# Third attention: its band added by a TensorE product into the scores' bank, in place of a VectorE add

## The chip, the cores and the metric

The kernel runs on one core of a Trainium2 chip. The metric is the device time of one execution in microseconds. The engines are TensorE (PE; its weight loads have a row of their own, PEld), VectorE (DVE), ScalarE (ACT), GpSimd (POOL) and SyncE (SP), which only issues transfers here. Each engine works through its own queue in order; semaphores tie them together.

## What is computed

A chain of six layers on 1024 tokens of 128 channels: a neighbourhood attention, a routed attention with a convolution, the attention that is changed, a mixture of eight experts, a full attention, and a second mixture. The third layer of work, cut to what matters:

```python
def _L2_attn_ref(x, Wqkv, Wproj, bproj):        # HEADS = 4, HEAD_DIM = 32, WIN = 128, RADIUS = 32
    xw = x.reshape(-1, WIN, C)                  # eight windows of 128 tokens
    q, k, v = ...                               # from xw @ Wqkv
    attn = einsum('bhid,bhjd->bhij', q, k) * SCALE
    attn = attn + band                          # 0 where 0 <= i - j <= 32, else -inf
    attn = softmax(attn, axis=-1)
    out = einsum('bhij,bhjd->bhid', attn, v)
    return out.reshape(...) @ Wproj + bproj
...
t = t + _L2_attn_ref(_ln_t(t), ...)
t = t + _L2_ffn_ref(_ln_t(t), ...)
```

## The kernel before

Tokens lie in T = 8 tiles of 128 (P). All semaphores and orders are written out by hand, one block for each engine; `at(name, k)` is the semaphore and the count that a wait wants, `.then_inc` raises it. `ps` is the whole PSUM, eight banks of 512 fp32 columns. Names that begin with `n2_` belong to the third attention.

Each engine has a loop over a step s for it, software-pipelined by hand. A tile's window is the tile itself, so a tile needs one score product per head: 4 heads x 128 columns fill one bank, `ps[:, s % 2]`. In step s the engines do this, in this order:

- PE: scores of tile s (four products, each fp32, which the trace shows as eight instructions), transpose of the normalised output of tile s-4 (L1085), transposes of the probabilities of s-2 (`turn4`, L865), product of the turned probabilities with the values of s-3, projection of s-5. Products are recorded at the helper's line L855.
- DVE: adds the band to the scores of tile s, out of the bank into the SBUF buffer `pS` (four slots in `arena`) (L1666), and takes the negated row maxima of it, into `nmx` (L1669); then normalises s-3 (reciprocal L1495, product L1496), adds the projection of s-5 to the residual (L1682), and gathers statistics for the next norm.
- ACT: four exponentials, one for each head, in place in `pS` with the maximum as bias (L734); then the copy of the turned output of s-4 (L670) and of the turned probabilities of s-2 (L743). All three stand in one queue.
- POOL: makes the four masked copies of the queries of a tile (L531), two slots, so those of tile t wait for the scores of tile t-2.

The semaphore `n2_sr` told PE that the add had read a bank, so the scores of s waited for the add of s-2. `n2_nmx` tells ACT of the maxima, `n2_p` counts exponentials, `n2_pt` turned tiles.

`band` is a 128x128 fp32 table of 0 and -1e30, made by POOL early; `ident` is the fp32 identity. `kr` is a 128x4x1024 buffer of rounded fp32 (fp32r) that holds the gathered keys in the second attention and parts of the first mixture later. POOL's queue ahead of the third attention is: last parts of the second attention (`split_stacks("n1")`), roots for the norms (L433), a wait for the gathered keys, the ones columns of the values (L561), then the first root of this attention's norm.

Of the kernel before, what the change touches and what calls it, by code (L numbers as in the profile page):

```python
# [5 lines left out]
P = 128  # L6
# [9 lines left out]
ALU = mybir.AluOpType  # L16
ACT = mybir.ActivationFunctionType
AX = mybir.AxisListType
# [5 lines left out]
NH4, HD4 = 4, 32  # L24
# [5 lines left out]
HEADS = T * NH8  # L30
# [121 lines left out]
def build(nc, A, out):  # L152
    with ExitStack() as ctx:
# [10 lines left out]
        def S(name):  # L164

            name = PLACE.get(name, (name, 0))[0]
            if name not in sems:
                sems[name] = ctx.enter_context(nc.semaphore(name))
            return sems[name]

        def at(name, k):

            return S(name), PLACE.get(name, (name, 0))[1] + k

        ps = ctx.enter_context(nc.psum_tensor("ps", [P, 8, HALF], F32))


        ident = sb("ident", [P, P])
        ones = sb("ones", [P, P])
        upper = sb("upper", [P, P])  # L180
        band = sb("band", [P, P])
# [110 lines left out]
        fills = sb("fills", [P, 1, P])  # L292


        q_high, k_stack, q_low, k_high = (kr[:, i, :] for i in range(4))
        k_masked = qr[:, :, :, :].rearrange("p b h n -> p (b h n)")

# [99 lines left out]
        def _(pool):  # L397
# [160 lines left out]
            split_stacks("n1")  # L558
            token_root("ln2", 0)
            pool.wait_ge(*at("k_gathered", KV * T))  # L560
            pool.memset(vaug4[:, :, :, HD4:HD4 + 1], 1.0).then_inc(S("ones_cols"), 1)  # L561
            pool.wait_ge(*at("ones_cols", 3))
            token_root("na", 0)
# [67 lines left out]
        def _(act):  # L631
# [97 lines left out]
            for s in range(T + 6):  # L729
                if s < T:  # L730
                    act.wait_ge(*at("n2_nmx", s + 1))
                    for h in range(NH4):
                        v = pS[:, s % 4, P * h:P * h + P]
                        act.activation(v, v, ACT.Exp, bias=nmx[:, s, h:h + 1]).then_inc(S("n2_p"), 1)  # L734
                t = s - 4
                if 0 <= t < T:
                    o_copy("n2", t, 6)
                t = s - 2
                if 0 <= t < T:
                    act.wait_ge(*at("n2_pt", t + 1))  # L740
                    if t >= 4:
                        act.wait_ge(*at("n2_pv", t - 3))
                    act.activation(pT[:, t % 4, :], ps[:, 2 + t % 2, :], ACT.Copy).then_inc(S("n2_pta"), 1)  # L743
# [109 lines left out]
        def _(pe):  # L853
# [218 lines left out]
            for s in range(T + 6):  # L1072
                if s < T:
                    pe.wait_ge(*at("n2_qm", s + 1))
                    if s >= 2:
                        pe.wait_ge(*at("n2_sr", s - 1))
                    for h in range(NH4):
                        mm(ps[:, s % 2, P * h:P * h + P], qm[:, s % 2, h, :],
                           bT[:, P * s:P * s + P]).then_inc(S("n2_s"), 1)
                t = s - 4  # L1080
                if 0 <= t < T:
                    pe.wait_ge(*at("n2_o", t + 1))
                    if t >= 1:
                        pe.wait_ge(*at("n2_oT", t))
                    pe.transpose(ps[:, 6, 0:P], oK[:, t % 2, :], ident[:, :]).then_inc(S("n2_ot"), 1)  # L1085
                t = s - 2
                if 0 <= t < T:
                    pe.wait_ge(*at("n2_p", NH4 * (t + 1)))
                    if t >= 2:
                        pe.wait_ge(*at("n2_pta", t - 1))  # L1090
                    turn4(2 + t % 2, [pS[:, t % 4, P * h:P * h + P] for h in range(NH4)]).then_inc(S("n2_pt"), 1)
                t = s - 3
                if 0 <= t < T:
                    pe.wait_ge(*at("n2_pta", t + 1))
                    if t >= 2:
                        pe.wait_ge(*at("n2_o", t - 1))
                    for h in range(NH4):
                        ins = mm(ps[:, 4 + t % 2, 33 * h:33 * h + 33], pT[:, t % 4, P * h:P * h + P], vaug4[:, t, h, :])
                    ins.then_inc(S("n2_pv"), 1)
                t = s - 5  # L1100
                if 0 <= t < T:
                    pe.wait_ge(*at("n2_oT", t + 1))
                    if t >= 1:
                        pe.wait_ge(*at("n2_add", t))
                    mm(ps[:, 7, 0:P], oT[:, P * t:P * t + P], w2p[:, :]).then_inc(S("n2_proj"), 1)
# [256 lines left out]
        def _(dve):  # L1362
# [297 lines left out]
            for s in range(T + 7):  # L1660
                if s < T:
                    dve.wait_ge(*at("n2_s", NH4 * (s + 1)))
                    if s >= 4:
                        dve.wait_ge(*at("n2_pt", s - 3))
                    v = pS[:, s % 4, :].rearrange("p (h k) -> p h k", h=NH4)
                    dve.tensor_tensor(v, ps[:, s % 2, :].rearrange("p (h k) -> p h k", h=NH4),  # L1666
                                      band[:, :].unsqueeze(1).broadcast_to([P, NH4, P]), ALU.add).then_inc(S("n2_sr"), 1)
                    dve.wait_ge(*at("n2_sr", s + 1))
                    dve.tensor_reduce(nmx[:, s, 0:NH4], v, AX.X, ALU.max, negate=True).then_inc(S("n2_nmx"), 1)  # L1669
                t = s - 6  # L1670
                if 0 <= t < T:
                    dve.wait_ge(*at("n2_add", t + 1))
# [278 lines left out]
```

## Time and profile before

| | |
|---|---|
| runs of the kernel, us | 543.63, 554.05, 555.6 |
| median, us | 554.05 |
| profiled execution, us | 544.95 |
| its span in the trace, us | 543.2 |
| mean granted TensorE clock, share of full | 0.937 |
| third attention's loop in the trace, us from the span's start | 271.6 to 303.2 |

Times in the rows are microseconds from the start of the span, durations are microseconds unless marked ns. A matmul's duration includes its way through the array, so matmuls that follow each other overlap in the rows: the distance of two starts is what a product costs in a row of products. The granted clock is 1.00 for 2.4 GHz and 0.50 for 1.2 GHz.

### The profile page before, as it was taken

What the parts mean: (1) busy time and instruction counts of PE and PEld (TensorE: products, weight loads), DVE (VectorE), ACT (ScalarE), POOL (GpSimd) and SP (SyncE); (2) the same over time, 40 slices, a digit from 0 to 9 for tenths busy, and PEclk for the clock granted to TensorE, in tenths of its full rate; (3) what the DMA queues carried; (4) which work ended last, traced back from release to release, by engine and by line L of the source; (5) the groups of instructions that cost most, each with busy time, mean ns of one, the idle gap of its engine ahead of it and who ended that gap; (6) DMA issues with size and microseconds to landing.
All of it is one profiled execution on the core that took longest, in us unless ns stands there. A gap on an engine that the chain in (4) does not pass through costs nothing.

```text
span 543.2 us, 9959 instructions
## 1 busy us (share of the span) xinstructions
PE 480.2 (88%) x3712; PEld 366.2 (67%) x3712; DVE 342.8 (63%) x863; ACT 251.8 (46%) x471; POOL 129.4 (24%) x168
## 2 busy tenths in 40 slices
PE   4989999595999999987489789999999899979994
PEld 4267776233778677764278569999999654567983
DVE  3988887388967978996465753333312761367367
ACT  0859887173544755471065175455541213310630
POOL 7332244013512232322350231111200500021000
PEclk9999999699899999997698569999999999979998
DMA  8000000000000000070000000111111000000001
GB/s 287 7 2 2 1 3 1 0 2 2 0 1 1 2 2 1 2 311 1 0 1 2 1 21 1 39 47 59 50 40 40 19 1 0 2 0 1 1 1 39
DMA packets 4681, 13.49 MB, mean 25 GB/s; under 512 B 466, under 2 KB 1562, under 8 KB 4250
## 3 DMA queue, kind: packets, MB, share of 16 engines
q1 hardware_dynamic: 4634, 12.86, 6.9%
q8 instruction: 30, 0.49, 0.4%
q14 instruction: 17, 0.14, 0.1%
HBM read 12.34 MB, written 0.52 MB: 24 GB/s over the span
## 4 chain that ended last, share of the span: by engine, by line
PE 74%; DVE 16%; ACT 3%; issue 3%; POOL 2%; DMA 1%; DVEq 0%; POOLq 0%; ACTq 0%
PE ps L855 63%; PE ps L865 9%; DVE tabs L1403 2%; DVE st L1387 1%; POOL rstd L433 1%; DVE pT L1487 1%; DVE tabs L1429 1%; PE ps L952 1%; DMA xT<-in_xT_dram 1%; ACT arena L734 1%; DVE nmx L1669 1%; DVE arena L1666 1%; DVE mv L1393 1%; DVE kr L1554 1%; DVE nmx L1622 1%
## 5 line engine op out<-in xcount | busy, mean ns | idle before, releaser
L855 PE MATMUL ps<-kr,qr 128*128 128x512 f32 (+2 forms) x368 | 115.3, 418 | 8.5 <-DVE vaug L1469 4.3
L855 PEld LDWEIGHTS ps<-kr,qr 128*128 128x128 f32 x368 | 69.7, 195 | 27.0 <-issue 7.6
L865 PE MATMUL ps<-ident,arena 128*128 128x128 f32 x474 | 75.5, 275 | 3.0 <-DVE pT L1487 1.6
L865 PEld LDWEIGHTS ps<-ident,arena 128*128 128x128 f32 x474 | 57.8, 141 | 15.6 <-issue 2.7
L769 ACT ACTIVATE arena<-ps,first 128x512 f32<-128x512 f32 x64 | 42.7, 688 | 38.9 <-PE ps L855 38.8
L855 PEld LDWEIGHTS ps<-fw,arena 128*128 128x128 f32 x512 | 58.3, 192 | 0.6
L855 PE MATMUL ps<-fw,arena 128*128 128x128 f32 x512 | 58.3, 275 | 0.0
L1744 DVE SCALAR_TENSOR_TENSOR aK<-ps,cw,aK 128x128 f32<-128x128 f32 x64 | 18.0, 345 | 63.6 <-PE ps L855 63.6
L665 ACT ACTIVATE pT<-ps 128x512 f32<-128x512 f32 (+2 forms) x64 | 33.8, 528 | 51.3 <-PE ps L865 50.6
L717 ACT ACTIVATE arena<-ps,nmx 128x512 f32<-128x512 f32 x64 | 42.4, 687 | 14.4 <-DVE nmx L1622 14.3
L1622 DVE TENSOR_REDUCE nmx<-ps 128x1 f32<-128x512 f32 x64 | 43.5, 681 | 8.1 <-PE ps L855 7.9
L1487 DVE COPY pT<-ps 128x512 f32<-128x512 f32 (+2 forms) x64 | 38.6, 603 | 8.1 <-PE ps L865 7.7
L496 POOL TENSOR_TENSOR qr<-fw,mask 128x1024 fp32r<-128x1024 f32 x16 | 30.6, 1912 | 44.7 <-PE ps L855 32.7
L693 ACT ACTIVATE arena<-arena,nmx 128x384 f32<-128x384 f32 (+1 forms) x64 | 35.2, 581 | 5.8 <-DVE nmx L1520 5.8
L1520 DVE CUSTOM_DVE_ANT_0 arena<-ps,tabs 128x384 f32<-128x384 f32 (+1 forms) x64 | 32.6, 518 | 7.2 <-PE ps L855 7.2
L433 POOL TENSOR_TENSOR rstd<-ve,nhalf 128x4 f32<-128x4 f32 x14 | 14.2, 1013 | 95.3 <-DVE ve L1396 95.1
L855 PE MATMUL ps<-pT,tabs 128*32 128x128 f32 (+1 forms) x544 | 33.4, 294 | 0.8 <-ACT pT L665 0.8
L855 PE MATMUL ps<-kr 128*128 128x512 f32 x76 | 31.3, 499 | 1.0 <-ACT kr L832 1.0
L510 POOL TENSOR_TENSOR tabs<-vaug,ones 128x151 f32<-128x151 f32 x32 | 14.1, 439 | 70.0 <-PE ps L855 48.3
L653 ACT ACTIVATE pT<-ps,lowbias,islow 128x512 fp32r<-128x512 f32 x32 | 24.8, 777 | 2.9 <-PE ps L855 0.6
L865 PE MATMUL ps<-ident,tabs 128*128 128x128 f32 x48 | 10.7, 364 | 15.6 <-DVE tabs L1403 15.0
L1554 DVE CAST kr<-arena 128x512 fp32r x32 | 23.2, 734 | 1.9 <-issue 1.5
(264 smaller groups left out, 825.4 us busy)
## 6 DMA issues: line engine op xcount, KB each, us to landing
fw<-in_m_w_dram SPq DMA_DIRECT2D x2, 2048.0 KB, 11.1
fw<-in_m_w_dram SPq DMA_DIRECT2D x16, 256.0 KB, 2.9
convw<-in_convw_dram SPq DMA_DIRECT2D x1, 1600.0 KB, 11.1
rows<-in_rows_dram SPq DMA_DIRECT2D x1, 584.0 KB, 6.8
xT<-in_xT_dram SPq DMA_DIRECT2D x1, 512.0 KB, 3.6
out_dram<-aK SPq DMA_DIRECT2D x2, 256.0 KB, 2.3
w<-in_w_dram SPq DMA_DIRECT2D x1, 448.0 KB, 7.6
late<-in_late_dram SPq DMA_DIRECT2D x1, 360.0 KB, 11.5
```

Source lines behind the costliest of these rows:

```text
L496: pool.tensor_tensor(qr[:, t % 2, :, :].rearrange("p (g a) n -> p g a n", a=2), qst[:, :, P * t:P * t + P].unsqueeze(2).broadcast_to([P, 4 ...
L653: act.activation(pT[:, u % 4, :].bitcast(F32R), ps[:, u % 4, :], ACT.Identity, bias=lowbias[:, layer, a, k:k + 1], scale=islow[:, a:a + 1] ...
L665: act.activation(pT[:, m % 8, 0:w], ps[:, 4 + m % 2, 0:w], ACT.Copy).then_inc(S(f"{name}_pta"), 1)
L693: act.activation(v, v, ACT.Exp, bias=nmx[:, t, h:h + 1], scale=-1.0).then_inc(S("n0_p"), 1)
L717: act.activation(pS8[:, n % 8, :], ps[:, n % N1_S, :], ACT.Exp, bias=nmx[:, n // NH8, n % NH8:n % NH8 + 1]).then_inc(S("n1_p"), 1)
L769: act.activation(hid(e)[:, c // 2, HALF * (c % 2):HALF * (c % 2) + HALF], ps[:, c % 4, :], func, bias=col("L2_ffn_b1", FC * e + c // 2)).t ...
L855: return pe.matmul(dst, lhsT, rhs, start=start, stop=stop, skip_group_check=True)
L865: ins = pe.transpose(ps[0:rows, bank, cols * j:cols * j + cols], src, ident[0:cols, 0:cols])
L1487: dve.tensor_copy(pT[:, m % 8, 0:w], ps[:, 4 + m % 2, 0:w]).then_inc(S(f"{name}_ptd"), 1)
L1520: dve.tensor_tensor_reduce(arena_s(t)[:, h, 0:w], ps[:, s % 4, 0:w], tab[:, h, :, :].rearrange("p l j -> p (l j)"), -1.0, FMAX, ALU.add, A ...
L1554: dve.tensor_copy(kfil[:, t % 2, :, P * j:P * j + P], kst[:, :, bass.ds(r * P, P)]).then_inc(S("k_gathered"), 1)
L1622: dve.tensor_reduce(nmx[:, s // NH8, s % NH8:s % NH8 + 1], ps[:, s % N1_S, :], AX.X, ALU.max, negate=True).then_inc(S("n1_nmx"), 1)
```

## The change

The band comes into the scores' bank by a product of its own, ahead of the four score products, which now accumulate onto it: stationary operand an fp32r copy of the identity, moving operand an fp32r copy of the band read four times over (512 columns). DVE takes the maxima straight from the bank. ACT's exponentials read the bank and write `pS`, so it is ACT that now waits for the `pS` slot to be free (`n2_pt`), and PE's scores of s wait for the exponentials of s-2 in place of the add. The two fp32r copies are made by POOL in `kr`, once, after the last score product of the second attention.

```diff
+        ident_r = kr[:, 0, 0:P]
+        band_r = kr[:, 0, P:2 * P]
...
             token_root("ln2", 0)
             pool.wait_ge(*at("k_gathered", KV * T))
+            pool.wait_ge(*at("n1_s", HEADS))
+            copy(ident_r, ident[:, :]).then_inc(S("n2_band"), 1)
+            copy(band_r, band[:, :]).then_inc(S("n2_band"), 1)
+            pool.wait_ge(*at("n2_band", 2))
             pool.memset(vaug4[:, :, :, HD4:HD4 + 1], 1.0).then_inc(S("ones_cols"), 1)
...
                     act.wait_ge(*at("n2_nmx", s + 1))
+                    if s >= 4:
+                        act.wait_ge(*at("n2_pt", s - 3))
                     for h in range(NH4):
-                        v = pS[:, s % 4, P * h:P * h + P]
-                        act.activation(v, v, ACT.Exp, bias=nmx[:, s, h:h + 1]).then_inc(S("n2_p"), 1)
+                        act.activation(pS[:, s % 4, P * h:P * h + P], ps[:, s % 2, P * h:P * h + P], ACT.Exp, bias=nmx[:, s, h:h + 1]).then_inc(S("n2_p"), 1)
...
                     pe.wait_ge(*at("n2_qm", s + 1))
+                    if s == 0:
+                        pe.wait_ge(*at("n2_band", 2))
                     if s >= 2:
-                        pe.wait_ge(*at("n2_sr", s - 1))
+                        pe.wait_ge(*at("n2_p", NH4 * (s - 1)))
+                    mm(ps[:, s % 2, :], ident_r, band_r.unsqueeze(1).broadcast_to([P, NH4, P]), stop=False)
                     for h in range(NH4):
                         mm(ps[:, s % 2, P * h:P * h + P], qm[:, s % 2, h, :],
-                           bT[:, P * s:P * s + P]).then_inc(S("n2_s"), 1)
+                           bT[:, P * s:P * s + P], start=False, stop=h == NH4 - 1).then_inc(S("n2_s"), 1)
...
                     dve.wait_ge(*at("n2_s", NH4 * (s + 1)))
-                    if s >= 4:
-                        dve.wait_ge(*at("n2_pt", s - 3))
-                    v = pS[:, s % 4, :].rearrange("p (h k) -> p h k", h=NH4)
-                    dve.tensor_tensor(v, ps[:, s % 2, :].rearrange("p (h k) -> p h k", h=NH4),
-                                      band[:, :].unsqueeze(1).broadcast_to([P, NH4, P]), ALU.add).then_inc(S("n2_sr"), 1)
-                    dve.wait_ge(*at("n2_sr", s + 1))
-                    dve.tensor_reduce(nmx[:, s, 0:NH4], v, AX.X, ALU.max, negate=True).then_inc(S("n2_nmx"), 1)
+                    dve.tensor_reduce(nmx[:, s, 0:NH4], ps[:, s % 2, :].rearrange("p (h k) -> p h k", h=NH4), AX.X, ALU.max, negate=True).then_inc(S("n2_nmx"), 1)
```

## Rows read from the trace of the kernel before

**Rows 1.** The page's chain that ended last, by engine, shares of the span.

```profile
PE 74%; DVE 16%; ACT 3%; issue 3%; POOL 2%; DMA 1%; DVEq 0%; POOLq 0%; ACTq 0%
```

**Rows 2.** Two stretches: length, busy time of each engine, granted clock, DMA.

```profile
271.60:293.80 22.20, 18.34 (x152) 17.12 (x152) 14.46 (x34) 14.60 (x44) 7.45 (x8) 1.00 0.01 2
293.80:303.20 9.40, 8.77 (x35) 7.08 (x34) 4.09 (x20) 1.43 (x4) 1.02 (x1) 0.50 0.00 0
```

**Rows 3.** Timeline of PE: start, duration, engine, line, operation [idle before].

```profile
271.65 2.02 PE L855 MATMUL ps<-bT,arena 128*128 128x128 f32 x16 [0.99 <-DVE arena L1467]
...
278.71 1.08 PE L855 MATMUL ps<-arena,pT 128*128 128x33 f32 x8 [1.12 <-ACT pT L743]
279.62 1.14 PE L855 MATMUL ps<-bT,arena 128*128 128x128 f32 x8
...
281.95 1.14 PE L855 MATMUL ps<-bT,arena 128*128 128x128 f32 x8
283.83 0.30 PE L1085 MATMUL ps<-ident,oK 128*128 128x128 f32 x1 [0.73 <-ACT oT L670]
...
285.53 1.06 PE L855 MATMUL ps<-bT,arena 128*128 128x128 f32 x8
286.42 0.27 PE L1085 MATMUL ps<-ident,oK 128*128 128x128 f32 x1
...
286.97 0.98 PE L855 MATMUL ps<-arena,pT 128*128 128x33 f32 x8
287.78 0.47 PE L855 MATMUL ps<-late,oT 128*128 128x128 f32 x2
288.09 1.06 PE L855 MATMUL ps<-bT,arena 128*128 128x128 f32 x8
...
292.21 0.30 PE L1085 MATMUL ps<-ident,oK 128*128 128x128 f32 x1 [0.69 <-ACT oT L670]
...
298.28 1.76 PE L855 MATMUL ps<-arena,pT 128*128 128x33 f32 x8
```

**Rows 4.** Timeline of DVE in step 4, the same columns.

```profile
280.80 0.69 DVE L1666 TENSOR_TENSOR arena<-ps,band 128x512 f32<-128x512 f32 x1 [0.46 <-PE ps L855]
281.52 0.69 DVE L1669 TENSOR_REDUCE nmx<-arena 128x4 f32<-128x512 f32 x1
```

**Rows 5.** Timeline of ACT in step 4, the same columns.

```profile
282.24 1.28 ACT L734 ACTIVATE arena<-arena,nmx 128x128 f32<-128x128 f32 x4 [1.85 <-DVE nmx L1669]
283.43 0.26 ACT L670 ACTIVATE oT<-ps 128x128 f32<-128x128 f32 x1
283.58 0.58 ACT L743 ACTIVATE pT<-ps 128x512 f32<-128x512 f32 x1
```

**Rows 6.** Groups by form: busy us, mean ns of one, idle before.

```profile
L1622 DVE TENSOR_REDUCE nmx<-ps 128x1 f32<-128x512 f32 x64 | 43.5, 681 | 8.1 <-PE ps L855 7.9
L717 ACT ACTIVATE arena<-ps,nmx 128x512 f32<-128x512 f32 x64 | 42.4, 687 | 14.4 <-DVE nmx L1622 14.3
...
L734 ACT ACTIVATE arena<-arena,nmx 128x128 f32<-128x128 f32 x32 | 10.2, 390 | 8.7 <-DVE nmx L1669 8.6
...
L453 POOL TENSOR_SCALAR onesr<-ones 128x128 fp32r<-128x128 f32 x1 | 0.3, 295 | 0.0
```

**Rows 7.** Timeline of PE in the second attention: two of the convolution's products.

```profile
229.35 0.42 PE L855 MATMUL ps<-kv_high,convw_high 128*128 128x512 f32 x1
229.60 0.42 PE L855 MATMUL ps<-tabs_parts,convw_high 128*128 128x512 f32 x1
```

**Rows 8.** Timelines of POOL, PE and DVE at the second attention's end.

```profile
233.34 0.16 POOL L561 MEMSET arena<- 128x32 f32 x1
...
239.39 0.51 PE L855 MATMUL ps<-kr,qr 128*128 128x512 f32 x1
...
241.05 1.01 POOL L433 TENSOR_TENSOR rstd<-ve,nhalf 128x4 f32<-128x4 f32 x1 [7.54 <-DVE ve L1396]
...
242.09 0.34 DVE L1403 TENSOR_SCALAR tabs<-aK,mv,rstd 128x128 f32<-128x128 f32 x1
```

## The prediction, made before the changed kernel had run

> **What bounds the kernel now.** I read the page first, its chain that ended last, by engine [rows 1]. TensorE (PE) holds 74% of that chain, VectorE (DVE) 16%, ScalarE (ACT) 3%. So a microsecond taken from DVE is worth something only where DVE sits on the chain. The third attention (the loops that count `n2_...`) is such a place. The stretches [rows 2] show it in two pieces. From 271.6 to 293.8 us PE runs at the full clock (2.4 GHz) and is busy for 18.3 of 22.2 us. From 293.8 to 303.2 us, when the last tiles drain, it runs at half (1.2 GHz) and is busy for 8.8 of 9.4 us. The first piece is what the change can touch: eight steps, one tile each.
>
> Then I read the timeline of each engine in that stretch, because an average hides that the eight steps have different limits. PE's order within a step s is scores of tile s, turned output (`ot`) of s-4, turned probabilities of s-2, product with values (`pv`) of s-3, projection of s-5. From the starts in [rows 3] the pitches, back to back, are: scores 0.89 (285.53 to 286.42), `ot` and turn together 0.55 (to 286.97), `pv` 0.81 (to 287.78), projection 0.31 (to 288.09). Their sum, 2.56 us, is the pure PE work of a step. But the score products of steps 4 to 7 start at 279.62, 281.95, 285.53 and 288.09: 2.82 us apart on average. The difference is holes: PE waits 1.12 us for ACT's copy of turned probabilities (before 278.71), 0.73 us for ACT's copy of the turned output (before 283.83), and again 0.69 us (before 292.21). What is late each time is a copy that ACT has queued behind the four exponentials of its step, and these wait for DVE. In step 4 the scores start at 279.62, DVE adds the band at 280.80 and takes the maximum at 281.52 [rows 4], ACT's exponentials start at 282.24, the copy of the output follows at 283.43 and that of the turned probabilities at 283.58 [rows 5]. So two limits are close together: PE's own work (2.56) and, in about every second step, the line scores, add, maximum, exponentials, copy.
>
> **What the change removes.** Eight DVE adds of 128x512. One add delays the maximum by 0.72 us (280.80 to 281.52) [rows 4]. The maximum stays and now reads the bank instead of the SBUF copy. The trace has that form: 128x512 out of `ps` is 681 ns in the second attention, and the present one is 0.69 [rows 4, 6]. I take no difference. So each line to the exponentials gets 0.72 shorter at DVE.
>
> **What it adds to PE.** Eight products of one identity with 512 columns of band, rounded operands (fp32r). The nearest rows are the convolution's products, also fp32r, 128x128 by 512, with a weight load each: they start 0.25 us apart at the full clock, 229.35 and 229.60 [rows 7]. I take 0.26. Bounds: below, 0.11, the pitch of one of the eight 128-column parts of the scores (0.89 / 8) [rows 3], since 512 columns can't pass faster than 128; above, 0.42, the whole duration of such a product, if it overlapped with nothing [rows 7]. The product stands ahead of the scores, so it is on PE's own queue and on the line to the maximum: the line gets 0.72 - 0.26 = 0.46 us shorter, PE's step 0.26 longer, 2.82 us. That is exactly the average step that the trace shows with its holes. This is the centre of the forecast: the holes are filled with band.
>
> **What it moves.** The exponentials read the bank. ACT from `ps` in this loop: a copy of 128x128 is 0.26, one of 128x512 is 0.58 [rows 5]; the exponential of 128x512 from `ps` with the same bias operand is 0.687 [rows 6]. 0.687 - (0.58 - 0.26) = 0.37 us for 128 columns from the bank, against 0.39 from the arena [rows 6]. I take no change (bounds 0.26, the bare copy, and 0.39). The Trainium skill, page "VectorE: DVE Perf Modes", section "The TRN2 errata", gives ScalarE 224 cycles of fixed cost from SBUF and 172 from PSUM, so 52 cycles or 43 ns less for each of the 32 exponentials; by that estimate the line to the copies would be 0.17 us shorter still in a step. The rows agree in the sign and show about half of it.
>
> **The wait that is added.** Scores of s waited for the add of s-2; now band and scores of s wait for the exponentials of s-2. Behind that wait on PE stand all of the step: scores, `ot`, turn of s-2, `pv`, projection. The turn of s-2 needs the same exponentials anyway, so only the scores lose their lead. In steady steps they have no use for it: the exponentials of s-2 end about 2.5 us before PE comes to the scores of s. At the start they do. With the same start at 271.65 [rows 3], working through the queues with the durations above:
> Step 0: scores reach DVE at 273.07, exponentials 273.80 to 275.08. Step 1: exponentials 275.04 to 276.32. Step 2: band waits for the first exponentials and starts at 275.2 (before, these scores ran ahead without asking for ACT); maximum 276.62, exponentials 277.35 to 278.63, turned copy of tile 0 ends at 279.12, so `pv` of tile 0 starts at 279.2 (278.71 before: 0.5 us late). Step 4: band at 280.02, scores 280.28, maximum 281.46, exponentials 282.2 (282.24 before), copies 283.38 and 283.53. Step 5: band 282.55, `ot` 283.78 (283.83 before), `pv` 284.33, projection 285.15. Step 6: band 285.46, scores 285.72, `ot` 286.61, projection 287.97. Step 7: band 288.28 (scores at 288.09 before), scores 288.54, `ot` 289.43, because its copy (288.99) is now in time; `pv` 289.98, exponentials of tile 7 end 291.65, its `ot` of tile 4 at 291.96 against 292.21 before.
> Sum of the loop: -0.25 us. Five band products lie on PE's own path (steps 3 to 7): at 0.42 each the sum is +0.55, at 0.11 it is -1.0.
>
> **The wait that is moved.** ACT now waits for the turn of tile s-4 before it writes the arena; that turn was issued two steps earlier, so it costs nothing. POOL makes the two rounded 128x128 copies before the ones columns and the third attention's first root. A POOL copy 128x128 to fp32r is 295 ns [rows 6]. It waits for the last score product of the second attention, which starts at 239.39 and lasts 0.51 [rows 8], so it runs from about 240.0 to 240.65; the memset (0.16, at 233.34 before) ends about 240.85, and the root starts at 241.05 in any case, because it waits for DVE [rows 8]. Cover: 0.2 us of slack. If it is gone, up to 0.3 us passes on, since DVE's first normalised tile starts at 242.09, right behind that root [rows 8]; the query splits come some 19 us later and their bias adds later too. PE's wait for the two copies ends 31 us before it is reached. I take 0.05 for POOL.
>
> **The sum.** -0.25 + 0.05 = -0.2 us: 544.95 becomes 544.75 for the profiled execution (span 543.2 and 1.75 around it). The runs shown are 543.63, 554.05 and 555.6: the median lies 9.1 us above the profiled execution, which is near the lowest. No row tells what makes the two levels, so I carry the difference over: 554.05 - 0.2 = 553.8 us.
>
> **Rivals.** A, the full saving reaches the end: 8 x 0.46 = 3.7 us, and the drain, where PE needs 1.67 us a tile at the full clock (0.55 + 0.81 + 0.31) but about twice that at half [rows 2, 3], keeps the full clock, some 3.5 us more. 554.05 - 7.2 = 546.9. For it: all the holes end on ACT behind DVE. Against: PE's own 2.82 a step stands in the way, and the clock fell at 293.8 in the first step without score products, which is still there. Chance 0.08.
> B, the lost lead costs more than the start: if semaphores and copies eat the margin, each of the steps 2 to 7 is held 0.3 to 0.7 us by exponentials of s-2. That is 2 to 4 us, 557. Against: the closed line of a tile, 0.26 + 1.09 + 0.73 + 1.28 + 0.1 = 3.5 us, serves two steps, 1.75 each, far below 2.82. Chance 0.12.
> C, the other side: the clock. PE now has holes of about 1.1 and 0.8 us near 274 and 278.4. If the clock falls there, as it fell at 293.8 after the first step without score products, and stays down, a step costs twice its 2.8 us: `pv` takes 1.76 instead of 0.98 [rows 3]. From four such steps on (11.2 us) the kernel is slower by over 2%; five make 14 us, 568. Against: a hole of 1.12 us stood there before [rows 3], and the clock held. Chance 0.05, of which 0.03 beyond four steps.
> The forecast itself, within 1.5 us of -0.2: 0.75.
>
> **Range and chances.** The mechanism alone gives 552.3 to 555.3 on the median's level. The two levels of the runs weigh more: if the median falls on the lower, 543.6 + the same. So the range is 542.8 to 557.0, which takes in B and A. Two per cent, about what a measurement of this kernel can tell from no change, is 11 us, more than half of the loop that is touched; only C or a change of level between the two kernels' runs gets there. Faster by over 2%: 0.04; within 2%: 0.91; slower by over 2%: 0.05.
>
> **What would show it.** Right: the score products' starts of steps 4 to 7 stay some 2.8 us apart with the holes before `ot` gone; the band product's pitch 0.25; the maximum 0.68 from the bank; first `pv` some 0.5 us later; DVE's busy time down by about 5.5 us and the end of the loop within 1 us. Wrong: steps of 2.6 us or less (A), holes before the band product in steps 4 to 7 (B), a granted clock of 0.5 before 290 us (C), or the root on POOL later than 241.4.

## The result

| | before | changed |
|---|---|---|
| median of 20 runs each, us | 545.03 (542.22 to 555.6) | 543.5 (539.41 to 555.0) |
| ratio | | 0.996, 95% interval 0.9943 to 0.9978 |
| profiled execution, us | 544.95 | 542.79 |
| its span, us | 543.2 | 541.0 |
| DVE busy, us | 342.8 | 337.4 |
| PE busy, us | 480.2 | 479.4 |

By these runs the changed kernel is 0.4% faster, 1.2 to 3.1 us, where the forecast was -0.2 us, no change. How much of that is the change's own is what the experiments are about. 543.5 us lies inside the stated range, and the kernel stays within 2%, but it moved, and the forecast said it would not. The ratio leaves out the longest executions of both kernels; the three of these that were traced (555.19 for the kernel before, 554.0 and 553.12 for the changed one) all show a long fall of the clock between about 440 and 464 us, which is the upper level of the three runs shown ahead of the prediction.

```profile
440.00:464.50 24.50, 24.50 (x44) 0.51 0.00 0
```

That is one stretch of such an execution of the kernel before: length, PE's busy time, granted clock 0.51 where it is 1.00 otherwise.

The loop of the changed kernel, PE's timeline (start, duration, operation, idle before):

```profile
270.17 0.47 PE L862 MATMUL ps<-kr 128*128 128x512 f32 x1 [0.94 <-issue]
...
273.58 0.47 PE L862 MATMUL ps<-kr 128*128 128x512 f32 x1 [0.93 <-ACT arena L741]
...
277.40 1.08 PE L862 MATMUL ps<-arena,pT 128*128 128x33 f32 x8 [0.46 <-ACT pT L750]
278.31 0.47 PE L862 MATMUL ps<-kr 128*128 128x512 f32 x1
278.62 1.05 PE L862 MATMUL ps<-bT,arena 128*128 128x128 f32 x8
...
280.87 0.48 PE L862 MATMUL ps<-kr 128*128 128x512 f32 x1
...
283.44 0.47 PE L862 MATMUL ps<-late,oT 128*128 128x128 f32 x2
283.66 0.47 PE L862 MATMUL ps<-kr 128*128 128x512 f32 x1
283.97 1.05 PE L862 MATMUL ps<-bT,arena 128*128 128x128 f32 x8
284.86 0.27 PE L1095 MATMUL ps<-ident,oK 128*128 128x128 f32 x1
...
286.44 0.48 PE L862 MATMUL ps<-kr 128*128 128x512 f32 x1
...
290.03 0.30 PE L1095 MATMUL ps<-ident,oK 128*128 128x128 f32 x1 [0.56 <-ACT oT L676]
```

`ps<-kr` is the band product. It starts at 278.31 in step 4, 280.87, 283.66 and 286.44 in step 7. Step 4 has no projection yet and takes 2.56 us; the two after it, which are whole steps, take 2.79 and 2.78. The holes ahead of the turned outputs in steps 5 and 7 [rows 3] are gone. What remains is a hole of 0.93 us before the third band product, the lost lead, and 0.46 and 0.56 us at both ends. DVE and ACT of step 4:

```profile
279.71 0.69 DVE L1673 TENSOR_REDUCE nmx<-ps 128x4 f32<-128x512 f32 x1 [0.69 <-PE ps L862]
```

```profile
280.44 1.14 ACT L741 ACTIVATE arena<-ps,nmx 128x128 f32<-128x128 f32 x4 [1.54 <-DVE nmx L1673]
281.46 0.29 ACT L676 ACTIVATE oT<-ps 128x128 f32<-128x128 f32 x1
281.61 0.62 ACT L750 ACTIVATE pT<-ps 128x512 f32<-128x512 f32 x1
```

The maximum from the bank takes 0.69 as before [rows 4]. The four exponentials take 1.14 us where they took 1.28 [rows 5]; one is 368 ns on average where it was 390 [rows 6], and they follow each other more closely too:

```profile
L741 ACT ACTIVATE arena<-ps,nmx 128x128 f32<-128x128 f32 x32 | 9.1, 368 | 8.9 <-DVE nmx L1673 8.9
```

Counted from its first product, the loop compares so (us; `ot` is the turned output, tile 4's is the first after the last scores):

| | forecast | changed | before |
|---|---|---|---|
| band or scores of step 4 | 8.37 | 8.14 | 7.97 |
| band or scores of step 7 | 16.63 | 16.27 | 16.44 |
| `ot` of tile 4 | 20.31 | 19.86 | 20.56 |
| last projection | | 29.78 | 30.69 |

So the loop gives 0.9 us. The two profiled spans differ by 2.2, and most of the rest stands ahead of the loop: it starts at 270.17 instead of 271.65 [rows 3], behind code that is the same but for POOL's two copies. The experiments begin with that.

### The profile page after: what moved, and what is told of

It reads as the page before. It is cut to its first block, busy times and chain, and to the rows that moved or that the text cites. A ratio compares the mean times of both kernels' runs of the same rounds, so it can differ in the third digit from the quotient of the medians.

```text
span 541.0 us, 9969 instructions
## 1 busy us (share of the span) xinstructions
PE 479.4 (89%) x3720; PEld 366.5 (68%) x3720; DVE 337.4 (62%) x855; ACT 251.1 (46%) x471; POOL 130.2 (24%) x170
## 4 chain that ended last, share of the span: by engine, by line
PE 73%; DVE 16%; ACT 3%; issue 3%; POOL 2%; DMA 1%; DVEq 0%; POOLq 0%; ACTq 0%
PE ps L862 63%; PE ps L872 9%; DVE tabs L1413 2%; DVE tabs L1439 2%; DVE st L1397 1%; POOL rstd L435 1%; DVE pT L1497 1%; PE ps L959 1%; DMA xT<-in_xT_dram 1%; ACT arena L741 1%; DVE mv L1403 1%; DVE kr L1564 1%; ACT arena L699 1%; DVE nmx L1632 1%; DVE st L1378 1%
## 5 line engine op out<-in xcount | busy, mean ns | idle before, releaser
L498 POOL TENSOR_TENSOR qr<-fw,mask 128x1024 fp32r<-128x1024 f32 x16 | 30.7, 1918 | 44.1 <-PE ps L862 32.6
L862 PE MATMUL ps<-kr 128*128 128x512 f32 x84 | 35.1, 497 | 2.9 <-ACT kr L839 1.0
L862 PEld LDWEIGHTS ps<-kr 128*128 128x128 f32 x84 | 15.3, 187 | 17.9 <-issue 14.7
```

The costliest lines, as they stand in the source:

```text
L498: pool.tensor_tensor(qr[:, t % 2, :, :].rearrange("p (g a) n -> p g a n", a=2), qst[:, :, P * t:P * t + P].unsqueeze(2).broadcast_to([P, 4 ...
L862: return pe.matmul(dst, lhsT, rhs, start=start, stop=stop, skip_group_check=True)
```

## The experiments

The changed loop and three theories were put to the test. M: the gain is the loop's alone, and the rest of the 2.2 us is the clock, which differs from execution to execution. N: there is a real gain outside the loop. P: after the change PE's own work limits steps 3 to 7; its rival Q, that the line over DVE and ACT still does.

**The two kernels again.** No edit.

> The changed kernel once more, beside the kernel before on one chip. Theory M (the gain is made in the third attention's loop alone, where the traces show 29.8 us from its first product to its last projection against 30.7): ratio 0.997 to 0.9995, 0.3 to 1.5 us. Rival N (there is a real gain outside the loop too, since the twenty runs gave 0.996, 2.2 us): 0.994 to 0.997. In the trace: band product on PE adds 0.22 us to the pitch of a step, four exponentials 1.14 us.

> The kernel before, once more, as one of the kernels compared, for the scatter of the times and for the clock. Theory K (the start of the loop and the clock in its drain differ from execution to execution of the same code): ratio 0.996 to 1.004; loop from first product to last projection 30.7 us if the clock falls about 22 us into it, 28.0 us if it holds, as it did with the copies alone. Rival (the drain's clock is set by the kernel): 30.7 us and a fall at 22 us again.

Measured: the changed kernel 0.9935 (0.9878 to 0.9992), the kernel before against itself 1.0012 (0.9984 to 1.004). The interval of the first holds both theories. The trace of the kernel before settles the start of the loop:

```profile
270.21 2.02 PE L855 MATMUL ps<-bT,arena 128*128 128x128 f32 x16 [0.99 <-DVE arena L1467]
```

It starts at 270.21, where the changed kernel's stood at 270.17. This execution took 543.45 us against 542.79: at an equal start the difference is 0.7 us, not 2.2. The clock is part of the cause of the two starts: in this execution, as in the changed kernel's, it is down from 251.4 to 254.8 us, in the first one of the kernel before from 249.4 to 256.3. But that gives only the last 0.5 of the 1.44 us. The same product, first execution and this one:

```profile
246.74 1.08 PE L855 MATMUL ps<-pT,tabs 128*32 128x128 f32 x32 [0.78 <-ACT pT L665]
```

```profile
245.80 1.08 PE L855 MATMUL ps<-pT,tabs 128*32 128x128 f32 x32 [0.78 <-ACT pT L665]
```

0.94 us stand between the two here already, and 0.47 at 93 us (93.51 and 93.04 for one product), before the clock's first fall in these traces, near 98 us. So the start is no work of the change, as M said, since two executions of one kernel show both; but only part of it is the clock's. That the drain would keep the clock at times is not seen here: the clock fell 22 us into the loop and the last projection started 30.74 us into it, as the rival said of this execution.

**The two copies alone.** Into the kernel before:

```diff
             pool.wait_ge(*at("k_gathered", KV * T))
+            pool.wait_ge(*at("n1_s", HEADS))
+            copy(ident_r, ident[:, :]).then_inc(S("n2_band"), 1)
+            copy(band_r, band[:, :]).then_inc(S("n2_band"), 1)
+            pool.wait_ge(*at("n2_band", 2))
```

> The kernel before with only POOL's wait and its two rounded copies added, used by nobody. Theory M: they are hidden, 0 to +0.3 us, and the first root of the third attention's norm starts within 0.1 us of where it did (241.05), measured from the second attention's last score product (239.39). Rival N, that the new wait shifts POOL's work and so gives the gain outside the loop: -0.5 to -1.3 us.

Measured 0.9991 (0.995 to 1.0031), the median 545.32 against 545.52: no gain, no loss. The first root of the norm starts 1.67 us after the second attention's last score product (243.07 and 241.40), where it was 1.66 before, as M said. In the changed kernel's own timeline of POOL the copies take 0.31 each, and the root then still idles 0.18 us for DVE:

```profile
239.13 0.31 POOL L455 TENSOR_SCALAR kr<-ident 128x128 fp32r<-128x128 f32 x1 [6.79 <-PE ps L862]
239.41 0.31 POOL L455 TENSOR_SCALAR kr<-band 128x128 fp32r<-128x128 f32 x1
239.77 0.16 POOL L567 MEMSET arena<- 128x32 f32 x1
240.11 1.01 POOL L435 TENSOR_TENSOR rstd<-ve,nhalf 128x4 f32<-128x4 f32 x1 [0.18 <-DVE ve L1406]
```

This trace gave something else: its loop, the same code as before, started at 272.92, kept the full clock through the drain and reached its last projection 28.04 us in, against 30.7. So the drain's clock is worth 2.65 us in the loop, and the kernel does not fix it: the second half of M. At the end of this execution 1.6 of them were gone again, though. From the last projection to the end it took 244.15 us, where the two executions of the kernel before took 242.61 and 242.50: the clock fell once more, from 328.9 to 332.3 us, in the first mixture, and stayed down longer near 480.

**The move without the product.** DVE still adds the band, in place in the bank:

```diff
-                    v = pS[:, s % 4, :].rearrange("p (h k) -> p h k", h=NH4)
-                    dve.tensor_tensor(v, ps[:, s % 2, :].rearrange("p (h k) -> p h k", h=NH4),
+                    v = ps[:, s % 2, :].rearrange("p (h k) -> p h k", h=NH4)
+                    dve.tensor_tensor(v, v,
                                       band[:, :].unsqueeze(1).broadcast_to([P, NH4, P]), ALU.add).then_inc(S("n2_sr"), 1)
```

with ACT's and PE's waits and the exponentials' source as in the change.

> DVE still adds the band, but in place in the bank; maximum and exponentials read the bank, scores of s wait for the exponentials of s-2. It has the move of the change without PE's product. Theory M1, that the exponentials from the bank were the part of the gain that the forecast left out: four exponentials take 1.14 instead of 1.28 us, each hole of PE behind them shrinks by 0.14, the lost lead costs 0.3 to 0.6 at the start; loop -0.5 to +0.3 us against before. Rival M2, the lost lead costs in every step: steps of 2.9 us or more, loop +1 to +3 us.

Measured 0.9999 (0.9954 to 1.0043). PE and ACT:

```profile
275.27 1.13 PE L856 MATMUL ps<-bT,arena 128*128 128x128 f32 x8 [1.89 <-ACT arena L735]
276.23 0.88 PE L866 MATMUL ps<-ident,arena 128*128 128x128 f32 x4
...
282.92 1.14 PE L856 MATMUL ps<-bT,arena 128*128 128x128 f32 x8
284.68 0.30 PE L1086 MATMUL ps<-ident,oK 128*128 128x128 f32 x1 [0.62 <-ACT oT L670]
```

```profile
275.31 1.14 ACT L735 ACTIVATE arena<-ps,nmx 128x128 f32<-128x128 f32 x4 [0.19 <-DVE nmx L1668]
```

The exponentials take 1.14 here as well, so that gain belongs to reading the bank. The hole of step 5 is 0.62 instead of 0.73 [rows 3], and the steps 4 to 7 start 2.33, 3.47 and 2.55 us apart, against 2.33, 3.58 and 2.56: M2, a cost in every step, falls. The sum of M1 (-0.5 to +0.3 us) can't be read from this trace, because the clock fell inside the loop. The lost lead is bare here, a hole of 1.89 us before the scores of step 2, because add and maximum still stand one behind the other; with the band on PE it is 0.93. In this execution the clock fell to half right behind that hole, from 276.4 to 279.8 us. That is how rival C of the prediction begins, in a kernel with a hole of 1.9 us; it came back after 3.4 us and did not reach C's four steps. It was seen once, and in none of the eight traces of the changed kernel, with 0.93. The execution took 550.61 us: it also had a fall from 440 to 457 us.

**The product twice.** Into the changed kernel:

```diff
                     mm(ps[:, s % 2, :], ident_r, band_r.unsqueeze(1).broadcast_to([P, NH4, P]), stop=False)
+                    mm(ps[:, s % 2, :], ident_r, band_r.unsqueeze(1).broadcast_to([P, NH4, P]), start=False, stop=False)
```

> The changed kernel with the band product issued twice into the same bank (the mask is -2e30 then). Theory P, PE is the limit of steps 3 to 7 after the change and a band product costs its pitch: 0.21 to 0.26 us more a step, loop +1.2 to +2.0 us against the changed kernel. Rival Q, PE still has slack in the loop and the line over DVE and ACT limits it: +0.2 to +0.6 us.

Steps 6 and 7 of it (the two products are one row, x2), and the first hole after them:

```profile
284.72 0.70 PE L862 MATMUL ps<-kr 128*128 128x512 f32 x2
285.26 1.05 PE L862 MATMUL ps<-bT,arena 128*128 128x128 f32 x8
...
287.73 0.70 PE L862 MATMUL ps<-kr 128*128 128x512 f32 x2
...
291.54 0.30 PE L1096 MATMUL ps<-ident,oK 128*128 128x128 f32 x1 [0.56 <-ACT oT L676]
```

The step is 3.01 us, 0.23 more than 2.78, and the turned output of tile 4 starts 21.23 us into the loop, 1.37 later: theory P, six times 0.23 (the first two products stand in the start's holes). The whole kernel did not show it: 0.9974 (0.9929 to 1.0019), median 543.96. In this trace the clock held through the drain and the last projection came at 28.56 us, earlier than the 29.78 of the changed kernel. From there to the end it took 244.08 us against 242.84, again with a fall near 327 us.

**The product left out.** The changed kernel without the band product, so the mask is missing from the computation.

```diff
-                    mm(ps[:, s % 2, :], ident_r, band_r.unsqueeze(1).broadcast_to([P, NH4, P]), stop=False)
...
-                           bT[:, P * s:P * s + P], start=False, stop=h == NH4 - 1).then_inc(S("n2_s"), 1)
+                           bT[:, P * s:P * s + P]).then_inc(S("n2_s"), 1)
```

> The changed kernel without the band product: the mask is left out of the computation, everything else (maximum and exponentials from the bank, waits) stays. Theory P (PE is the limit after the change): each of steps 3 to 7 is 0.22 us shorter, the turned output of tile 4 starts 0.9 to 1.6 us earlier in the loop than with the band (19.86 us into it). Rival Q (the line over DVE and ACT limits it): 0.2 us or less there, with holes before the turned outputs in place of the band.

```profile
285.93 1.06 PE L862 MATMUL ps<-bT,arena 128*128 128x128 f32 x8
...
288.49 1.06 PE L862 MATMUL ps<-bT,arena 128*128 128x128 f32 x8
```

The step is 2.56 us, PE's pure work without the band, and the turned output of tile 4 starts 18.55 us in: 1.31 earlier. P again, from the other side. The line over DVE and ACT has room for 2.56. Ratio to the kernel before 0.9948 (0.9907 to 0.9988). The traced execution, 548.64 us, kept the clock in the drain and had a fall from 438.5 to 455.5 us.

**Both.** The kernel before with the product added, and DVE still adding the band.

```diff
                         pe.wait_ge(*at("n2_sr", s - 1))
+                    mm(ps[:, s % 2, :], ident_r, band_r.unsqueeze(1).broadcast_to([P, NH4, P]), stop=False)
                     for h in range(NH4):
                         mm(ps[:, s % 2, P * h:P * h + P], qm[:, s % 2, h, :],
-                           bT[:, P * s:P * s + P]).then_inc(S("n2_s"), 1)
+                           bT[:, P * s:P * s + P], start=False, stop=h == NH4 - 1).then_inc(S("n2_s"), 1)
```

> The kernel before with the band product added on PE, and DVE still adding the band and writing the arena (mask -2e30): the cost side of the change alone. Theory M: the product lies on the line of a step and in PE's own work, so the turned output of tile 4 starts 0.7 to 1.8 us later in the loop than before (20.56). Rival R (the forecast's picture that the product only fills holes): 0.3 us or less.

```profile
290.20 0.30 PE L1094 MATMUL ps<-ident,oK 128*128 128x128 f32 x1 [0.28 <-ACT oT L676]
...
292.98 0.30 PE L1094 MATMUL ps<-ident,oK 128*128 128x128 f32 x1 [0.92 <-ACT oT L676]
```

The turned output of tile 4 starts 21.49 us in, 0.92 later than in the kernel before: theory M. R falls. The holes in front of the turned outputs stay, because the product lengthens the line just as it lengthens PE's work. What fills the holes in the change is not the product; it is that DVE's add and part of the exponentials leave the line. From this kernel to the changed one the same mark moves from 21.49 to 19.86: 1.6 us is what the DVE add and the SBUF reads were worth, and 0.9 is what the product costs. The difference is the loop's 0.7. The kernel's time shows nothing of the cost, 0.9995 (0.9966 to 1.0025); its loop too kept the clock in the drain.

**The drain filled.** The changed kernel with two idle products in each drain step, into a bank nobody reads:

```diff
+                elif s < T + 6:
+                    if s < T + 2:
+                        pe.wait_ge(*at("n2_p", NH4 * (s - 1)))
+                    for _ in range(2):
+                        mm(ps[:, s % 2, :], ident_r, band_r.unsqueeze(1).broadcast_to([P, NH4, P]))
```

> The changed kernel with two more products of identity and band in each of the six drain steps, into a bank that nobody reads. Theory K2: they keep PE busy, the clock stays at its upper level through the drain, and the last projection starts 27 to 29 us into the loop instead of 29.8; ratio to before 0.990 to 0.996. Rival: the clock falls at 22 us all the same, the products then cost up to 0.9 us a step, last projection at 31 to 34 us.

> The changed kernel with the filled drain once more: three of its seven timed executions took 539.5 to 539.8 us, the profiled one 542.65 with its loop starting at 273.2. Theory K: an execution of 539.5 to 540.6 us starts its loop near 270.2 and reaches the last projection 27.2 us later. Rival: the loop start is elsewhere, and the short executions gain outside the loop.

Measured 0.9929 (0.991 to 0.9949, seven executions) against the kernel before, 3.9 us, median 540.58: the fastest of all. In both traces the clock holds and the last projection starts 27.17 and 27.18 us in. The second execution took 540.8 us and its loop started at 271.41, so the theory of a start near 270.2 is not borne out by it; the changed kernel in an execution that started at 271.43 took 543.93. The drain of the two, changed kernel first:

```profile
292.68 0.47 PE L862 MATMUL ps<-late,oT 128*128 128x128 f32 x2
293.44 0.40 PE L1095 MATMUL ps<-ident,oK 128*128 128x128 f32 x1 [0.30 <-DVE oK L1506]
293.64 1.06 PE L872 MATMUL ps<-ident,arena 128*128 128x128 f32 x4
294.49 1.76 PE L862 MATMUL ps<-arena,pT 128*128 128x33 f32 x8
```

```profile
292.90 0.71 PE L862 MATMUL ps<-kr 128*128 128x512 f32 x2
293.44 0.32 PE L1100 MATMUL ps<-ident,oK 128*128 128x128 f32 x1
293.60 0.60 PE L872 MATMUL ps<-ident,arena 128*128 128x128 f32 x4
294.04 0.98 PE L862 MATMUL ps<-arena,pT 128*128 128x33 f32 x8
```

Both turn an output at 293.44. The idle products sit in a hole, and the product with the values behind it takes 0.98 instead of 1.76.

**The same in the kernel before.** Into the kernel with the two copies alone:

```diff
+                elif s < T + 6:
+                    if s < T + 2:
+                        pe.wait_ge(*at("n2_sr", s - 1))
+                    for _ in range(2):
+                        mm(ps[:, s % 2, :], ident_r, band_r.unsqueeze(1).broadcast_to([P, NH4, P]))
```

> The kernel before (band added by DVE) with the same two products in each drain step, and the two copies on POOL that they need. Theory M: the clock holds, last projection 28.0 us into the loop; ratio to before 0.994 to 0.997, and the changed kernel with the filled drain stays 0.7 to 1.2 us faster than this one. Rival N (the changed loop has a further gain of over 1 us apart from the drain's clock): 2 us or more between the two.

Measured 0.9981 (0.9962 to 0.9999). The clock held, the last projection came 28.05 us in. In the loops the two filled kernels differ by 0.87 us (28.05 and 27.18), the same as the unfilled ones. But the ratio misses M's 0.994 to 0.997: here the same products bring 1 us, in the changed kernel 3. Against their kernels before the two filled kernels stand at 0.9929 and 0.9981, 2.8 us apart, each with an interval of about 1.1 us to either side, where M said 0.7 to 1.2. That speaks for more than the loop in the timed runs, as N said. The traces place part of it behind the loop: from the last projection to the end this kernel took 243.58 us, the changed one 242.32 and 242.21, and near 480 us the clock was down for 10.2 us here (478.4 to 488.6) and for 6.8 us there. That is one trace; why the fall was longer is not shown.

**Filled as far as the first mixture.** In addition 28 products of 256 columns ahead of PE's waits for the next norms:

```diff
+            warm(6, 5)
             for i in range(2):
...
+                warm(5, 5)
...
             router("m2", 0, 4, oT, "nb_T", range(4, T))
+            warm(12, 5)
```

> The kernel with the filled drain, and 28 products of 256 columns on operands that lie there anyway, put before PE's waits for the next norms and for the first mixture. Theory K2: the clock stays at its upper level from 270 to the first mixture's products, whose first 5 us ran at the lower one; 2 to 4 us less than with the filled drain alone, ratio to before 0.984 to 0.990. Rival: the products delay the turns, or the clock falls between the bursts; within 1 us of the filled drain (0.993).

Measured 0.9971 (0.9944 to 0.9998), 2.3 us slower than the filled drain alone, though the two intervals meet: neither theory's ratio. The clock did hold at 1.00 from the loop to beyond 330 us, and still the mixture did not start earlier:

```profile
298.33 2.75 PE L862 MATMUL ps<-first 128*128 128x256 f32 x12
...
308.64 5.43 PE L862 MATMUL ps<-first 128*128 128x256 f32 x24
313.72 1.51 PE L862 MATMUL ps<-kr,qr 128*128 128x512 f32 x5
```

Six such products take 2.75 us, 0.46 each, and twelve 5.4. The mixture starts 16.15 us after the last projection, instead of 13.2 to 13.3 with the filled drain alone and 13.6 without: the filling outlasted the waits. The idea is not refuted by it; a filling of half the size was not run.

**More executions of the two kernels.** No edit, to see which clock goes with which time.

> The changed kernel in another execution, to see its clock. Theory K: in executions of about 539.5 us (lower than any of the kernel before) the clock holds through the drain and the last projection starts 27.1 to 27.3 us into the loop; in those of about 542.7 it falls 22 us into it and that is 29.8. Rival: the short executions gain elsewhere, the loop's length is 29.8 in all.

> The same once more, same expectations: 27.1 to 27.3 us from the first product to the last projection where the drain's clock holds, 29.8 where it falls at 22 us.

> The changed kernel in another execution. Theory K (each execution's clock pattern decides the rest): at about 539.5 us the drain's clock holds, the last projection starts 27.2 us into the loop; at 542.7 the loop starts near 270.2 and it is 29.8; at 543.9 the loop starts near 271.5 and it is 29.8. Rival: an execution of 539.5 us with 29.8 us.

> The same in another execution, same expectations: 27.2 us into the loop where the time is about 539.5, 29.8 where it is 542.7 or more.

> The same in another execution, same expectations: 27.2 us into the loop where the time is about 539.5, 29.8 where it is 542.7 or more.

> The changed kernel in one more execution. Three patterns of the clock have been seen, told apart by the start of the loop: near 270.2, 271.5 and 273.2 us. If an execution of about 539.5 us is met, theory K says loop start near 270.2 and the clock held through the drain (27.2 us to the last projection).

> The kernel before in another execution. Theory K: at 543.5 us the loop starts near 270.2, at 545 near 271.6, at 542.2 the drain's clock holds (28.0 us from first product to last projection instead of 30.7).

All traces without a fall after 440 us and without idle products, in order of the loop's start (us). The last column is the execution less the two before it:

| kernel | loop starts | to last projection | execution | the rest |
|---|---|---|---|---|
| changed, again | 270.03 | 29.83 | 542.61 | 242.75 |
| changed, 3 | 270.13 | 29.77 | 542.74 | 242.84 |
| changed | 270.17 | 29.78 | 542.79 | 242.84 |
| before, again | 270.21 | 30.74 | 543.45 | 242.50 |
| product twice | 270.31 | 28.56 | 542.95 | 244.08 |
| changed, 4 | 270.48 | 29.71 | 543.12 | 242.93 |
| changed, 7 | 271.43 | 29.75 | 543.93 | 242.75 |
| both | 271.49 | 28.81 | 544.02 | 243.72 |
| changed, 5 | 271.54 | 29.76 | 544.14 | 242.84 |
| before | 271.65 | 30.69 | 544.95 | 242.61 |
| copies alone | 272.92 | 28.04 | 545.11 | 244.15 |

Three more executions had the long fall: changed 271.08, 29.83, 554.0 and 273.17, 27.19, 553.12; before 271.66, 30.72, 555.19. The starts lie in three groups, 270.0 to 270.5, 271.4 to 271.8 and 272.9 to 273.2, and one, 271.08, by itself. The drain kept the clock in every loop of the third group. In the first two, the unedited loops of both kernels lost it each time, but the two loops with more products kept it, at starts of 270.31 and 271.49, and so did the move without the product (271.36), whose clock had fallen earlier in the loop. So the start alone does not decide; what does is not shown. Where an unfilled drain kept the clock, 1.1 to 1.6 us of the gain were given back: the rest is 243.7 to 244.2 us in place of 242.5 to 242.9.

At the same start the changed kernel is 0.7 us faster: without the time ahead of the loop its six executions take 272.50 to 272.64 us, the two of the kernel before 273.24 and 273.30. The loop gives 0.9, and 0.2 are lost behind it. No trace shows an execution near 539.5 us, of which the twenty runs of the changed kernel had three and those of the kernel before none.

## Why the prediction was wrong, point by point

The step that failed is the sum of the loop, -0.25 us. Its mechanism held in the main: PE's own work becomes the limit and the holes before the turned outputs go. Its terms were mis-sized: the exponentials were put at no change and took 0.14 us less a step, the band product was put at 0.26 and costs 0.22. Up to the turned output of tile 4, where the schedule ended, the loop gave 0.70 us, and 0.9 at its end, of which 0.7 reached the end of the kernel. What the twenty runs show above that, up to 2.2 us, has no term in the forecast at all (last point).

The picture of "holes filled with band" held only in part. With the band on PE and DVE's add left in place (both), the holes stay. They go because the line over DVE and ACT got shorter.


- **What bounds the loop: right.** PE's pure work and the line over DVE and ACT are close together, the holes before the turned outputs go, and PE's step becomes the limit. The step was 2.78 us for a forecast of 2.82; one product more makes it 3.01, one less 2.56.
- **The exponentials, "I take no change": wrong, the larger mis-sized term.** Four took 1.14 instead of 1.28 us, 0.14 a step. I compared the durations of single instructions (0.37 and 0.39) and left out that four in a row also follow each other faster. The rule weighed in the prediction (the Trainium skill, "VectorE: DVE Perf Modes", "The TRN2 errata") gave an estimate of 0.17; the trace agrees with it to 0.03. In the schedule it counts twice at the start: third band product 3.41 us in for a forecast of 3.55, first product with values 7.23 for 7.55.
- **The band product, "I take 0.26": 0.22 to 0.23.** The starts show 0.31 from band to scores, but the projection before it is followed after 0.22 where it was 0.31 ahead of scores [rows 3], so a step grows by 2.78 - 2.56 = 0.22. Three steps give 0.13 us between steps 4 and 7 (8.13 for a forecast of 8.26).
- **The sum: -0.25 to the turned output of tile 4, measured -0.70.** The terms above make the difference: 0.23 before step 4, 0.13 to step 7, 0.09 behind it. In the first drain steps another 0.2 us came, which the schedule did not go on to. Most of it lies right behind the turned output of tile 4: the transposes of the probabilities follow it after 0.28 us in the kernel before (292.21 [rows 3] to 292.49) and after 0.14 in the changed one (290.03 to 290.17). What they waited for was not traced further.

```profile
292.49 0.63 PE L865 MATMUL ps<-ident,arena 128*128 128x128 f32 x4
```

```profile
290.17 0.61 PE L872 MATMUL ps<-ident,arena 128*128 128x128 f32 x4
```

- **The lost lead: right in kind.** It costs the start (a hole of 0.93 before the third band product, first product with values 0.17 us later in the loop, 0.5 forecast) and nothing in steady steps. The margin was smaller than the "about 2.5 us" of the prediction, whose own schedule gives 2.0 for step 6: the exponentials of s-2 end 2.1 and 2.3 us before the band product of steps 6 and 7. It was enough. Rival B falls.
- **POOL, 0.05: right.** Hidden, 0.18 us to spare for 0.2 forecast.
- **Rival A, the full saving: not that.** 3.7 us would have needed PE's 2.82 to yield. But its second half, the drain's clock, is real and worth 2.6 us in the loop: six traces with an unfilled drain had it (one of the changed kernel, and the copies alone, the move without the product, the product twice, the product left out, both), and all four with idle products. Where the unfilled ones can be compared, 1.1 to 1.6 us of it did not reach the end.
- **Rival C, the clock falling at the start: not in the changed kernel, seen once with a hole of 1.89 us, and then for 3.4 us.**
- **The level, 553.8: wrong by a step that had no ground.** Three runs gave a median of 554.05 and I carried it over; twenty give 545.03. The level is a clock event near 440 us that either kernel can meet.
- **What stays open.** At equal starts the gain is 0.7 us, 0.13%. The repeats' intervals (0.9878 to 0.9992 and, of the changed kernel's eight further executions, 0.9951 to 0.9994) hold that; the twenty runs' (0.9943 to 0.9978) does not, and the filled kernels stand 2.8 us apart instead of 0.9. The mean granted clock on record for each execution shows where the rest comes from. Of the changed kernel's 33 executions under 550 us, 12 have 0.946 or 0.949 and take 539.4 to 542.7 us. Of the kernel before, 62 under 550 us have their clock on record, and one reaches 0.944 (542.09 us); all others lie lower. (The twenty runs of the kernel before have no clock on record; two of them, 542.22 and 542.25 us, are as short as that one.) Without these 12 and that one, the means are 543.6 and 544.7 us, about 1 us apart; with them 542.8 and 544.6. So the changed kernel meets a better course of the clock more often, and there is a gain beyond the loop's own, as theory N said. Why it does, and where in the execution the clock is kept, no trace shows, because no such execution was traced. The four of 0.949 (539.4 to 540.0 us) have the granted clock of the traces with a filled drain (0.949 and 0.950). 542.7 less the drain's 2.6 is 540.1, so a drain that kept its clock would explain them, if nothing of it were given back behind the loop, as it was in the product twice (start 270.31, 542.95 us). That is argued, not shown.

## What to carry to other kernels

When an engine is taken out of a line, go on with the schedule to the last instruction of the loop and put in the pace of several instructions in a row, not the duration of one: a few tenths of a microsecond, counted over the loop, are as much as this whole change brought, 0.7 us or 0.13%. Before a profile pair is read as a gain, compare the starts of a stretch whose code is the same in both: 1.5 of the 2.2 us stood there. A stretch that got shorter is not yet a gain either: read the time behind it too, where 1.1 to 1.6 us of a kept clock were lost again. And where TensorE drains a pipeline at half clock, a few idle products in the holes are cheap: 12 of them brought 3 us in the changed kernel, over four times what the change did, and 1 us in the kernel before.

## What the runs showed of the hardware

The loop's start lies in three groups in nineteen of the twenty traces, whatever the kernel (270.0 to 270.5, 271.4 to 271.8, 272.9 to 273.2 us), and each group has its own course of the clock ahead of the loop: down near 252 us from 251 to 255, from 249 to 256, or from 254 to 257. A drain at the lower clock (`pv` 1.76 instead of 0.98 us) costs 2.6 us over six steps; when it was kept without idle products, another fall of some 3.4 us came near 330 us in the three traces that had no fall after 440 us. A fall from about 440 to 464 us, in the middle of products that leave PE no hole (busy 24.5 of 24.5 us), costs some 10 us (543.93 and 544.14 against 553.12 and 554.0 for the changed kernel); nothing in the traces shows what sets it off. ACT's exponentials of 128 columns follow each other 0.26 us apart from PSUM and 0.30 from SBUF ((1.14 - 0.37) / 3 and (1.28 - 0.39) / 3).
